# Moving a token permutation from the vector engine's access patterns to TensorE's transposes and weight loads

## What is computed

```python
h = take(W.T, x) + b + positions
u = layernorm(h)
Bu = einsum('blh,ph->blp', u, B_bar)              # complex, 64 states
xs = associative_scan(x_t = Lambda_bar * x_(t-1) + Bu_t)   # along the 256 positions of a sequence
ys = 2 * einsum('blp,hp->blh', xs, C_tilde).real + D * u
h = h + gelu(ys)
xn = layernorm(h)
cw = softmax over the top 2 of (router_w xn + router_b), zero elsewhere
y_e = fc2_e(silu(fc1a_e xn) * fc1b_e xn)
out = h + sum over e of cw_e * y_e
```

## Time and profile before

| | us |
|---|---|
| median of three runs | 178.87 |
| the three runs | 177.69, 178.87, 178.97 |
| the profiled execution, its own time | 180.08 |
| span of the profiled execution, first to last instruction | 178.3 |
| mean granted TensorE clock in the span | 0.837 of full |

### The profile page before, as it was taken

The page is one execution under the profiler, slowest core; times in us unless marked ns, Lnnn a source line. Parts: engine busy times, 40 slices in busy tenths (PEclk is TensorE's granted clock), DMA queues, the critical chain, the costliest instruction groups (busy, mean ns, idle before and its releaser), DMA issues.

```text
span 178.3 us, 3561 instructions
## 1 busy us (share of the span) xinstructions
PE 124.3 (70%) x791; PEld 103.8 (58%) x791; DVE 123.7 (69%) x498; ACT 72.1 (40%) x230; POOL 96.4 (54%) x118
## 2 busy tenths in 40 slices
PE   0003564955957967594999999999999999993000
PEld 0001224825925836583898789898888989892000
DVE  1898999599999589868447755666677776741084
ACT  2015270272065006028333456575656666562000
POOL 5777787000067677537624777777664646556000
PEclk9999996596597597557556999999999999999555
DMA  3311129150042134034223113443421011100594
GB/s 100 99 44 46 51 71 194 69 179 0 6 159 93 47 85 184 30 89 106 67 56 88 51 63 83 111 118 96 111 77 38 23 32 36 41 29 14 170 375 161
DMA packets 13430, 15.57 MB, mean 87 GB/s; under 512 B 3020, under 2 KB 9430, under 8 KB 13411
## 3 DMA queue, kind: packets, MB, share of 16 engines
q1 hardware_dynamic: 9458, 8.17, 17.1%
q0 software_dynamic: 2784, 5.28, 9.3%
q10 hardware_dynamic: 1168, 1.90, 3.2%
HBM read 9.53 MB, written 6.27 MB: 89 GB/s over the span
## 4 chain that ended last, share of the span: by engine, by line
PE 36%; DVE 5%; DMA 5%; issue 3%; POOL 1%; DVEq 1%; ACTq 0%; POOLq 0%; ACT 0%
PE bank L1078 9%; PE bank L1064 9%; PE bank L1054 8%; PE bank L1044 5%; DMA yres<-results 4%; PE bank L1080 3%; DMA results<-ysb,dest 1%; POOL results L365 1%; PE bank L950 1%; DVE act_h L679 1%; PE bank L927 1%; DVEq L665 1%; DVE ysum L754 1%; DVE res L757 1%; ACTq L883 0%
## 5 line engine op out<-in xcount | busy, mean ns | idle before, releaser
L354 POOL DMA_INDIRECT sorted_rows<-rows,slot x32 | 34.3, 1071 | 34.4 <-DVE slot L581 25.6
L679 DVE SCALAR_TENSOR_TENSOR act_h<-bank,w1b,sil 128x128 f32<-128x128 f32 x78 | 23.7, 346 | 11.3 <-PE bank L1064 11.3
L668 DVE COPY w1b<-w_sb 128x516 f32 x39 | 20.5, 526 | 14.6 <-DVE act_h L679 7.4
L365 POOL DMA_INDIRECT results<-ysb,dest x22 | 21.6, 982 | 15.8 <-ACT ysb L862 14.7
L1078 PE MATMUL bank<-w_sb,act_h 128*128 x156 | 25.5, 288 | 0.4
L1064 PE MATMUL bank<-xT,w1b 128*128 128x128 f32 x156 | 25.3, 287 | 0.1
L1054 PE MATMUL bank<-xT,w1b 128*128 128x128 f32 x156 | 25.3, 287 | 0.0
L850 ACT ACTIVATE sil<-bank,w1b 128x128 f32<-128x128 f32 x78 | 24.4, 364 | 1.1 <-PE bank L1054 1.1
L1054 PEld LDWEIGHTS bank<-xT,w1b 128*128 128x128 f32 x156 | 23.8, 215 | 0.1
L841 ACT COPY xT<-bank 128x128 f32<-128x128 f32 x39 | 10.3, 264 | 31.8 <-PE bank L1044 30.6
L365 POOL DMA_INDIRECT results<-ysb,xt x17 | 17.0, 1003 | 11.2 <-ACT ysb L862 7.6
(11 more groups left out here) (217 smaller groups left out, 221.4 us busy)
## 6 DMA issues: line engine op xcount, KB each, us to landing
w_sb<-w_all SPq DMA_DIRECT2D x8, 386.0 KB, 3.6
xt<-sorted_rows SPq DMA_DIRECT2D x39, 65.0 KB, 1.9
yres<-results SPq DMA_DIRECT2D x4, 256.0 KB, 4.8
yres<-results ACTq DMA_DIRECT2D x4, 256.0 KB, 5.7
sorted_rows<-pad SPq DMA_DIRECT2D x1, 520.0 KB, 6.2
sorted_rows<-rows,slot POOLq DMA_INDIRECT x32, 2.4
out<-res SPq DMA_DIRECT2D x2, 256.0 KB, 2.6
out<-res ACTq DMA_DIRECT2D x2, 256.0 KB, 2.1
```

The lines of the kernel that those rows point to most:

```text
L354: gp.indirect_dma_start(sorted_rows[:, :], bass.IndirectOffsetOnAxis(ap=slot[:, k, t:t + 1], axis=0), rows[:, k, t, :], None).then_inc(s_s ...
L365: gp.indirect_dma_start(results[:, :], bass.IndirectOffsetOnAxis(ap=target, axis=0), ysb[i][:, :], None, bounds_check=bound, oob_is_err=Fa ...
L668: v.tensor_copy(w1b[i % 4][:, :], w_sb[:, bass.ds(at, W1)]).then_inc(s_wb, 1)
L679: v.scalar_tensor_tensor(act_h[i % 2][:, q], ps_l[sides(i)][:, q], w1b[i % 4][:, 2 * HID + 2 + c:2 * HID + 3 + c], sil[i % 2][:, q], ALU.a ...
```

## The change

The columns of `uT` are now in time order. `turn_u` writes tile j to every fourth column of the PSUM bank, beginning at column j, so a step of 16 bytes between the columns that one transpose writes. `b_times_u` is untouched. All of DVE's instructions in `scan` read and write contiguously. `outputs` loads as weights every fourth column of `zrot` and of `uT`, again 16 bytes apart. No instruction, wait or semaphore is added or taken away, and no order changes.

```diff
-            def in_time(ap):
-                return ap.rearrange("p (b q j) -> p b q j", b=2, j=GT)
-
-            def by_tile(ap):
-                return ap.rearrange("p (j b q) -> p b q j", j=GT, b=2)
+            def by_batch(ap):
+                return ap.rearrange("p (b t) -> p b t", b=2)
 
             def both(ap):
-                return ap.rearrange("p (q j) -> p q j", j=GT)[:, None, :, :].to_broadcast([P, 2, SEQ // GT, GT])
+                return ap[:, None, :].to_broadcast([P, 2, SEQ])
...
-                begin(v.tensor_tensor(in_time(rot[:, 0, :]), by_tile(ps_v[:, :]), cos_b, ALU.mult))
+                begin(v.tensor_tensor(by_batch(rot[:, 0, :]), by_batch(ps_v[:, :]), cos_b, ALU.mult))
                 dve.wait_ge(s_bu, 2 * g + 2)
-                v.tensor_tensor(in_time(rot[:, 1, :]), by_tile(ps_vs[:, :]), sin_b, ALU.mult).then_inc(s_rotin, 1)
+                v.tensor_tensor(by_batch(rot[:, 1, :]), by_batch(ps_vs[:, :]), sin_b, ALU.mult).then_inc(s_rotin, 1)
...
-                v.tensor_tensor(by_tile(zrot[:, 0, :]), in_time(zst[:, :]), cos_b, ALU.mult).then_inc(s_zrot, 1)
-                v.tensor_tensor(by_tile(zrot[:, 1, :]), in_time(zst[:, :]), sin_b, ALU.mult).then_inc(s_zrot, 1)
+                v.tensor_tensor(by_batch(zrot[:, 0, :]), by_batch(zst[:, :]), cos_b, ALU.mult).then_inc(s_zrot, 1)
+                v.tensor_tensor(by_batch(zrot[:, 1, :]), by_batch(zst[:, :]), sin_b, ALU.mult).then_inc(s_zrot, 1)
...
+                by_time = ps_uT[:, :].rearrange("p (q j) -> p j q", j=GT)
                 for j in range(GT):
                     pe.wait_ge(s_un, GT * g + j + 1)
-                    ins = te.transpose(ps_uT[:, j * P:(j + 1) * P], un[:, j, :], ident[:, :])
+                    ins = te.transpose(by_time[:, j, :], un[:, j, :], ident[:, :])
...
+                z = zrot[:, :, :].rearrange("p c (q j) -> p c j q", j=GT)
+                u = uT[:, g % 2, :].rearrange("p (q j) -> p j q", j=GT)
                 for j in range(2 * h, 2 * h + 2):
                     q = ps_y[h][:, (j % 2) * P:(j % 2 + 1) * P]
-                    te.matmul(q, zrot[:, 0, j * P:(j + 1) * P], cmat[:, 0, :], start=True, stop=False)
-                    te.matmul(q, zrot[:, 1, j * P:(j + 1) * P], cmat[:, 1, :], start=False, stop=False)
-                    ins = te.matmul(q, uT[:, g % 2, j * P:(j + 1) * P], diag[:, :], start=False, stop=True)
+                    te.matmul(q, z[:, 0, j, :], cmat[:, 0, :], start=True, stop=False)
+                    te.matmul(q, z[:, 1, j, :], cmat[:, 1, :], start=False, stop=False)
+                    ins = te.matmul(q, u[:, j, :], diag[:, :], start=False, stop=True)
```

## The result

The changed kernel is slower: 181.07 us in the median of 14 runs against 178.97 us in 14 runs of the kernel before, a ratio of 1.0117 with a 95% interval of 1.0085 to 1.015. That is +2.1 us where the prediction had -1.85 (177.0 us; the result lies outside its range of 175.4 to 179.4).

What follows compares the result with a forecast made beforehand. Until 84 us a DVE-PE-ACT ring, once per group, was taken as the bound, then PE alone. DVE's -2.58 us plus 0.73 us for loads gave -1.85 us, so 178.87 became 177.0 us, range 175.4 to 179.4.

Steps and rivals of the forecast that it cites:

- DVE's reads and writes: In scan: PSUM reads save 0, contiguous writes of zrot save 0.64 us a group, 2.58 us over four groups.
- the ring: Before 84 us, once per group: scan on DVE, outputs on PE, gelu on ACT, addition on DVE; savings there all count.
- The transposes' step in PSUM: PE's sixteen transposes writing PSUM with a 16-byte step: cost taken as 0, upper bound under half a microsecond.
- the idle time named as cover: ACT's 0.49 us idle after copying uT, before normed_x of group 0, said to hide a slower last transpose.
- The weight loads: 96 strided loads in outputs: about 0.205 us each, hidden at half clock, 0.09 us each at full, 0.73 us in all.
- The slack of group 1: DVE busy after gelu ends in group 1: 0.42 us, said to cover 0.36 us of load cost.
- The rival with DVE's write rate: Loads in outputs at 1.73 ns per element, 0.222 us each: 1.7 us in all, so 178.0 us; chance 0.08.
- How many loads meet the full clock: Records of outputs at full clock: 8 in group 2, 3 or 4 in group 1, none in groups 0 and 3.
- The rival on the clock: Clock rise in the expert loop moves by one tile, 1.8 us either way; later gives 178.8 us, chance 0.10.
- That the loop starts earlier by what the ring saves: At the handover to the expert loop: its start, tables and scatters all shift 1.85 us earlier.
- The signs of being wrong: Half-clock product over 0.48 us (27 ns a record), DVE's pair staying at 0.89, or earlier zrot without earlier gelu.
- The rival that ended on the slower side: Penalty adds to each of 24 loads a group, 88 ns each: +5.4 us, so 184.3 us; chance 0.12 in whole or part.

Runs made afterwards that it cites:

- e1: Changed kernel with outputs loading contiguous columns again; median 175.26 us, ratio 0.9793 to the kernel before.
- e4: Changed kernel with token numbers and position table laid in tile order, PE and DVE accesses contiguous, last stores in 512-byte pieces; 176.04 us, ratio 0.986.
- e3: Changed kernel with the transposes writing PSUM contiguously again; median 180.69 us, ratio 1.0113 to the kernel before.
- x1: Kernel before with weight loads of steps 1 to 4 side by side; records at full clock 0.113, 0.118, 0.173 and 0.228 us.
- e2: Kernel before with only the loads of outputs strided by four columns; median 182.31 us, ratio 1.0184.

## Why the prediction was wrong

*DVE's reads and writes.* Right: 0 for the reads, 0.64 us a group for the writes, on the ring. With contiguous loads (e1 and e4) the ring ends at 76.05 us in the mean against 78.92 in the three traces of before, 2.9 us earlier, of which 2.6 are this and the rest lies within what the clock does there.

*The transposes' step in PSUM.* Right in its sum of 0: e3 shows no difference. The mean of a turned tile went from 350 to 365 ns (L897, now L895), and is 337 in e3; part of such differences can be the clock, as single ones range from 272 to 477 ns in all three. Whether the idle time named as cover was what hid them was not tried.

*The weight loads.* This is the step that failed. "About 1.6 ns" per element, from DVE's L571, was mis-sized: x1 gives 1.8 ns per line, and with this step every column is a line of its own. The difference is small (0.205 against 0.234 us a record) but it lies across the threshold on which the sum hung. At half clock the text had the load "hidden (0.205 under 0.21)"; it is not. The product grew from 0.427 to 0.467 us, and the 84 half-clock records each pay 0.020, together 1.7 us. At full clock the price is 0.12 instead of 0.09. The slack of group 1 (0.42 us) was then too small for its loads: 20 x 0.020 + 4 x 0.12 = 0.88. By the predicted trace's own counts the sum should have been 64 x 0.020 + 8 x 0.12 + (0.88 - 0.42) = 2.7 us against 2.58 of gain, +0.1, and the trace after shows +0.24 at the end of the ring. That the two are so close is in part luck: in group 1 of the changed kernel DVE waits 0.18 us for gelu, not 0.46. The rival with DVE's write rate, 1.73 ns, was nearly this one; it got a chance of 0.08 and a price of 1.7 us.

*What the right rate does not explain.* It moves the forecast from -1.85 to +0.1, to 179.0 us, which is still inside the stated range. The measured +2.1 needs 2.0 us more, and they come from the next two steps as far as they are known.

*How many loads meet the full clock.* The count of 8 and 3 to 4 was read from a single trace and taken as fixed. The second trace of before has more of them and ends the ring 1.1 us earlier. Averaged over three traces the ring loses 0.9 us, not 0.1 or 0.2. The rival on the clock had said that no edit drives it. No run shows what drives it, but the change takes away what the ring wins from a full clock, and that had no term.

*That the loop starts earlier by what the ring saves.* The handover between them is not rigid: 4.7 us in both traces of before, 5.2 and 5.5 in those of the changed kernel, and equal (4.98) once the clock is held up. These 0.65 us are the clock's, and e2 (4.73 with strided loads) and e4 (5.52 with contiguous ones) speak against the loads as their cause. So 0.9 us of the 2.1 are shown to be the ring's; the other 1.2, at the handover and in the loop, stay open.

*The signs of being wrong.* A product at half clock was to take over 0.48 us if the gain was used up, 27 ns a record. It took 0.467, 20 ns, and yet the gain was gone: that sign left out the records at full clock, and over all 96 the price is (84 x 0.020 + 12 x 0.12) / 96 = 32 ns. And the duration of the loads, 0.33 us at half clock before and after, could not tell the rivals apart there.

*The rival that ended on the slower side.* Its place was right (the 24 loads a group), its mechanism wrong: the penalty does not come on top of the pitch, it is a floor under the load.

## What to carry to other kernels

Price a strided float32 weight load by the 16-byte lines that it touches, here 1.8 ns each for 128 columns on 128 partitions and steps up to 4, and hold that against the matmul it hides behind at both clocks; an estimate taken from another engine that comes within a few per cent of a threshold is no cover. A permutation that costs on whichever engine does it is best removed at the edges of the kernel, in the order in which the inputs are laid and the outputs stored. And where a clock moves between two levels at its own moments, read counts "at full clock" from more than one trace before a sum leans on them.

## What was not expected of the hardware

A float32 weight load with a step of 12 bytes is free at half clock (0.214 us a record against 0.213) and costs half as much again at full clock (0.173 against 0.113). A full clock can thus be worth nothing to loads: the products of outputs with a step of 16 bytes take 0.47 us at 1.2 and at 2.4 GHz. And 12 identity products whose results nobody reads, placed where TensorE waits ahead of the loop, were worth 178.56 - 176.72 = 1.8 us by the medians, or 0.5% by the ratio (0.1% to 0.9%). In that trace the clock is 1.00 from 80 us to beyond 102; the first trace of before has 0.50 from 84 until 96 (the earlier trace rows show the end of it), its second trace 1.00 from 78 until 96 without any such products and then a fall.
